# Splitting one GpSimd power into two, and twenty unread identity matmuls ahead of a tile's transposes, in a conv-attention and expert kernel

## The reference

```python
x = _L0_conv_ref(x, ...)        # group norm, qkv, 4-head softmax attention over 1024 pixels, residual
t = _to_tokens(x)               # 2 x 1024 tokens of 128 channels
t = t + _L1_attn_ref(_ln_t(t), ...)   # linear attention, 8 heads
t = t + _L1_ffn_ref(_ln_t(t), ...)    # the experts
```

```python
probs = softmax(xt @ Wr + br)
top_p, top_idx = top_k(probs, 2);  weights = top_p / top_p.sum(-1)
xn = (xt - mu) * rsqrt(var + 1e-5)
xe = xn * ln_g[e] + ln_b[e]
y  = gelu(xe @ W1[e] + b1[e]) @ W2[e] + b2[e]
out = sum over the two experts of weights * y
```

## Time and profile before

| | us |
|---|---|
| median of 3 runs | 366.21 (363.61, 366.21, 366.22) |
| the profiled execution | 364.42 |
| its span, first to last instruction | 362.7 |
| mean granted TensorE clock, share of full | 0.939 |

### The profile page before, as it was taken

One profiled execution on the slowest core, in us unless ns is written; L12 is line 12 of the kernel. 1 busy time (PEld: TensorE's weight loads), 2 busy tenths in 40 slices (PEclk: granted clock), 3 DMA queues, 4 the chain that ended last, 5 costly groups with the idle time before them and its releaser, 6 DMA issues.

```text
span 362.7 us, 6245 instructions
## 1 busy us (share of the span) xinstructions
PE 315.6 (87%) x1885; PEld 192.7 (53%) x1885; DVE 198.9 (55%) x617; ACT 194.1 (54%) x303; POOL 113.8 (31%) x190
## 2 busy tenths in 40 slices
PE   7979899999999998999999987697635499999996
PEld 3533433433333334435453254486534399999995
DVE  1586434474554844556447854766862057786510
ACT  1470566666666663656558620476532177777722
POOL 2073094000000000100030588007177835566540
PEclk9995989999999999999999999898858589999999
DMA  7069795744000005300000011300011422224215
GB/s 195 4 130 206 157 203 233 202 137 184 2 1 4 1 2 143 91 0 2 1 2 0 31 45 37 75 1 17 14 44 51 110 53 77 68 69 126 94 50 213
DMA packets 20541, 27.88 MB, mean 77 GB/s; under 512 B 3832, under 2 KB 14509, under 8 KB 20253
## 3 DMA queue, kind: packets, MB, share of 16 engines
q1 hardware_dynamic: 15800, 17.57, 18.1%
q0 software_dynamic: 3520, 9.39, 8.2%
q10 hardware_dynamic: 1188, 0.53, 0.6%
HBM read 11.15 MB, written 8.33 MB: 54 GB/s over the span
## 4 chain that ended last, share of the span: by engine, by line
PE 67%; DVE 12%; POOL 9%; issue 7%; ACT 3%; DMA 1%; DVEq 0%; POOLq 0%; ACTq 0%
PE ps L885 15%; PE ps L1104 9%; PE ps L1084 9%; POOL expert_in L507 7%; PE ps L847 7%; PE ps L866 5%; DVE above L1217 4%; PE ps L727 2%; PE ps L827 2%; PE ps L943 2%; PE ps L767 2%; PE ps L799 2%; PE ps L1063 1%; DVE pm L1220 1%; PE ps L958 1%
## 5 line engine op out<-in xcount | busy, mean ns | idle before, releaser
L575 ACT ACTIVATE probs<-ps 128x1024 f32<-128x1024 f32 x64 | 65.3, 1021 | 34.7 <-PE ps L866 34.6
L885 PE MATMUL ps<-probs,vT 128*32 128x512 f32 x256 | 68.3, 609 | 0.1
L885 PE MATMUL ps<-probs,ones 128*32 128x512 f32 x256 | 68.3, 609 | 0.0
L1217 DVE CUSTOM_DVE_ANT_0 above<-ps,above 128x512 f32<-128x512 f32 x56 | 38.7, 690 | 39.8 <-PE ps L847 38.0
L443 POOL TENSOR_TENSOR rstd<-ve,minus_half 128x1 f32<-128x1 f32 (+2 forms) x6 | 10.3, 1724 | 152.6 <-DVE ve L1259 83.3
L1084 PE MATMUL ps<-w,GT 128*128 x312 | 44.5, 288 | 9.8 <-ACT GT L705 9.5
L1104 PE MATMUL ps<-XTT,w1s 128*128 128x128 f32 x312 | 45.2, 292 | 4.3 <-issue 4.2
L513 POOL DMA_INDIRECT token_out<-Y,yidx x39 | 37.7, 966 | 33.1 <-DVE Y L1530 27.2
L568 ACT ACTIVATE above<-ps 128x512 f32<-128x512 f32 x56 | 33.6, 599 | 25.6 <-PE ps L827 25.6
L1084 PEld LDWEIGHTS ps<-w,GT 128*128 128x128 f32 x312 | 40.1, 201 | 11.5 <-issue 11.4
L866 PE MATMUL ps<-Qs,Ks 98*128 98x512 f32 x128 | 43.9, 424 | 0.7 <-issue 0.7
(11 more groups left out here) (221 smaller groups left out, 431.3 us busy)
## 6 DMA issues: line engine op xcount, KB each, us to landing
XR<-expert_in SPq DMA_DIRECT2D x39, 65.0 KB, 1.9
Qs<-q_hi SPq DMA_DIRECT2D x16, 128.0 KB, 2.7
w<-in_L_ffn_W SPq DMA_DIRECT2D x1, 2048.0 KB, 8.3
w<-in_L_ffn_W SPq DMA_DIRECT2D x8, 256.0 KB, 4.4
YG<-token_out SPq DMA_DIRECT2D x8, 256.0 KB, 3.9
Ks<-k_hi SPq DMA_DIRECT2D x14, 128.0 KB, 2.9
expert_in<-zeros POOLq DMA_DIRECT2D x1, 1300.0 KB, 5.5
expert_in<-zeros POOLq DMA_DIRECT2D x1, 1235.0 KB, 8.0
```

What stands on the lines that cost most here:

```text
L575: nc.scalar.activation(probs[:, s % 3, :], bank(2 + 2 * (s % 2), 2), ACT.Exp).then_inc(exp_done, 1)
L885: last = nc.tensor.matmul(bank(6 + o % 2)[i * HD:(i + 1) * HD, :], w, probs[:, s % 3, hd * HALF:(hd + 1) * HALF], start=kt == 0, stop=kt = ...
L1217: nc.vector.tensor_tensor_reduce(above[:, n % 2, :], bank(base), above[:, n % 2, :], scale=1.0, scalar=-3.0e38, op0=ALU.add, op1=ALU.max, ...
```

## The change

Three things are done.

1. `rsqrt` issues one instruction of 8 values for each row instead of one instruction of 16 values for two rows. Each raises `rstd_ready` by one, so the waits count further: `v_gates` waits for the first row alone, `v_shift` for the second.
2. Image 1's indirect transfers are counted on two semaphores, the first eight on one and the last eight on another. SP waits for both before tile 9, as before.
3. TensorE, behind `down(8)` and ahead of the transposes of tiles 9 and 10, waits for `slots` of both images and for the first eight transfers of image 1, and then issues `keep_busy(20, 0)`, into bank 0.

```diff
+    WARM = 20
@@
-        scattered = [sem(f"scattered{b}") for b in range(B)]
+        scattered = [sem(f"scattered{i}") for i in range(B + 1)]
@@ SP
                 if t in (0, OWN):
-                    sp.wait_ge(scattered[int(t == OWN)], 16 * 2 * J)
+                    if t == 0:
+                        sp.wait_ge(scattered[0], 16 * 2 * J)
+                    else:
+                        sp.wait_ge(scattered[1], 16 * J)
+                        sp.wait_ge(scattered[2], 16 * J)
@@ GpSimd, rsqrt
-                nc.gpsimd.tensor_tensor(rstd[:, i:i + rows, 0:columns], ve[:, i:i + rows, 0:columns],
-                                        minus_half[:, 0:rows, 0:columns], ALU.pow).then_inc(rstd_ready, 1)
+                for r in range(i, i + rows):
+                    nc.gpsimd.tensor_tensor(rstd[:, r, 0:columns], ve[:, r, 0:columns], minus_half[:, 0, 0:columns],
+                                            ALU.pow).then_inc(rstd_ready, 1)
@@ GpSimd, scatter
-                                                X2[:, b, j, :], None).then_inc(scattered[b], 16)
+                                                X2[:, b, j, :], None).then_inc(scattered[b + b * (2 * j // J)], 16)
@@ TensorE, expert_step
                 if s == OWN:
                     down(s - 1)
+                    pe.wait_ge(slots_ready, B)
+                    pe.wait_ge(scattered[1], 16 * J)
+                    keep_busy(WARM, 0)
                     x_transpose(s)
                     x_transpose(s + 1)
@@ DVE, norm_apply
-                dve.wait_ge(rstd_ready, n + 1)
+                dve.wait_ge(rstd_ready, n + 1 + (n - B) // 2)
@@ DVE, v_shift
-                dve.wait_ge(rstd_ready, B + 2 * b + 2)
+                dve.wait_ge(rstd_ready, B + 3 * b + 3)
@@ DVE, v_gates
-                dve.wait_ge(rstd_ready, B + 2 * b + 2)
+                dve.wait_ge(rstd_ready, B + 3 * b + 2)
```

## The result

| | before | after |
|---|---|---|
| median, us | 366.22 (363.61 to 366.39, 4 runs) | 371.66 (371.26 to 373.60, 4 runs) |
| profiled execution, us | 364.42 | 371.58 |
| its span, us | 362.7 | 369.8 |
| mean granted clock | 0.939 | 0.949 |

The ratio is 1.0176, 95% interval 1.0119 to 1.0234: slower by more than the 1% that can be told from no change. It is that of the means of the executions, 372.05 and 365.61, which differ by 6.4 us; the two medians alone differ by 5.4 us, a ratio of 1.015. The forecast was 370.1 us, the range 366.5 to 373.5.

What follows compares the result with a forecast made beforehand. The chain was 67% TensorE, which idled 9.20 us for tile 9's rows and restarted at half clock. Power -0.55, later transposes +8.0 and warm clock -2.4 gave +5.0 on 365.1: 370.1 us, range 366.5 to 373.5.

Steps and rivals of the forecast that it cites:

- The twenty matmuls: TensorE behind tile 8: 0.86 us each, 17.2 us in all, delaying tile 9's transposes from 285.8 to 293.8, +8.0 us.
- such a late return: Rival's small form: the full clock returns late, some 3 us of the twenty run at half; 371.6 us, nearly all of 6%.
- The warm clock: Tile 9's transposes to tile 11's first product at full clock: 4.15 us against 6.5 before, a gain of 2.4 us.
- T + 3.1: T is the start of tile 9's transposes; ACT's gelu for tile 9 was to end 3.1 us after it.
- The Trainium skill's rule: Prices a throttled stretch at length times one minus the clock's share; behind the gap 3.1 us back, sum +4.3 us.
- the reason that I gave: From tile 9's transposes: ACT's and DVE's steps lie between TensorE's and gain nothing from its clock, so 2.4 us, not 3.1.
- The power apart: Image 1's logits: first row ready 1.26 us earlier, but DVE's shift waits for the second, so slots come 0.55 us earlier.
- my base of 365.1 us: Mean of the four executions of the kernel before, to which the forecast added its +5.0 us.
- the cover: Rival at the gap before tile 9: a matmul costs 0.43 us, twenty end before the rows; some 362.2 us, 5%.
- fell in the twenty: Rival: the clock falls or starts at half in the twenty matmuls; 371.6 us, or some 390 if half throughout; 6%.
- lost behind them: Rival: the twenty run as priced but tile 9's transposes at half clock, 2.4 us not given back; 372.5 us, 4%.
- The last case: Rival: first eight transfers land late, the twenty start late, or the power gives no head start (then 370.7 us); 2%.

Runs made afterwards that it cites:

- ten_two: Changed kernel with ten identity matmuls instead of twenty, plus two single ones in TensorE's gaps in image 1's routing; median 362.28 us, 0.9900 of the kernel before.
- twenty_only: Changed kernel with the power of 16 values in one instruction as before, the twenty matmuls kept; median 373.50 us, 1.0204 of the kernel before.

## Why the prediction was right

**The twenty matmuls: right, but for their start.** I priced one at 0.86 us from the attention product's rows and they cost 0.867. The place behind tile 8, the free wait for the eighth transfer, the full clock throughout and the in-order wait of the transposes came as written. The distance grew by 8.20 us against +8.0. Within it a term that I had put at nothing is 0.4 us: behind the idle time of the routing the clock came back later than before. Tile 8's second product stands 7.30 us behind tile 5's, before 6.90, and the twenty start that much later. Before, the clock was back in the stretch from 272 to 273, some 3 us behind the start of tile 5's second product (269.12); here it is some 4 us behind (270.19):

```profile
273.00:274.00 1.00, 1.00 (x7) 1.00 (x7) 0.00 (x0) 0.00 (x0) 0.84 (x1) 0.50 0.20 67
274.00:275.00 1.00, 1.00 (x10) 1.00 (x10) 0.82 (x2) 0.15 (x1) 0.69 (x2) 0.98 0.21 67
```

I had named such a late return for the twenty themselves, and not for the tiles ahead of them. The experiments with 10, 14, 20 and 30 show that what counts is what lies past the landing, in full.

**The warm clock: right in mechanism, 0.5 us too large.** It gave 1.85 us and not 2.4; every kernel whose matmuls reach the landing, or end less than 0.8 us ahead of it, has 4.67 to 4.73 us from the transposes to tile 11, those without a warm clock 6.4 to 6.6. The term that I mis-sized is the way of tile 9 through DVE. I had the gelu end at T + 3.1, and it ends here:

```profile
298.56 0.63 ACT L711 ACTIVATE GT<-H 128x512 f32<-128x512 f32 x1 [1.21 <-DVE H L1551]
```

That is 299.19, T + 3.54. DVE began its addition at 297.83, when the first product had ended at 297.69: 2.2 us behind the transposes and not 1.8. The Trainium skill's rule (TensorE: Matmul & The Clock Gate, Terms) would have given back 3.1 us; the measured 1.85 lies further from it than my estimate. The trace agrees with the reason that I gave: TensorE waits for ACT twice in these 4.67 us, 0.50 and 0.53 us.

**The power apart: the wrong step.** I wrote that the distance from the power to the first transfer shrinks by 0.55 us, held at that by the second row on DVE. It changed by +0.08 in this execution and by -0.3 to +0.1 in all with the split and no extra matmuls. The rows of GpSimd and DVE do look as forecast, beside the earlier trace rows:

```profile
246.82 3.28 POOL L449 TENSOR_TENSOR rstd<-ve,minus_half 128x8 f32<-128x8 f32 x2 [19.34 <-DVE ve L1270]
```

```profile
248.59 0.22 DVE L1359 TENSOR_TENSOR lg<-ps,rstd 128x64 f32<-128x64 f32 x1 [0.34 <-POOL rstd L449]
...
250.13 0.17 DVE L1350 SCALAR_TENSOR_TENSOR nm<-lmv,rstd 128x8 f32<-128x8 f32 x1 [0.54 <-POOL rstd L449]
250.95 0.69 DVE L1551 TENSOR_TENSOR H<-ps,b1T 128x512 f32<-128x512 f32 x1 [0.65 <-issue]
```

The logits wait 0.34 us instead of 1.60, the shift 0.54, and tile 3's addition stands 4.13 us behind the power instead of 4.70. But that wait isn't what holds the routing. I stopped at DVE, and didn't follow the counts, for which DVE waits, back to TensorE. There, in the changed kernel:

```profile
255.47 2.04 PE L1113 MATMUL ps<-XTT,w1s 128*128 128x128 f32 x8 [0.68 <-issue]
...
257.84 0.63 PE L1008 MATMUL ps<-mask,ones 128*128 128x64 f32 x2
```

The product starts 1.2 us earlier relative to the power than before and takes 0.9 us longer. The clock had fallen at 253 to 254 after TensorE's gaps in the routing, where before it had fallen at 251 to 252 and was full again at 255 to 256. The clock's rows there, two of the kernel before and then one of this:

```profile
251.00:252.00 1.00, 0.66 (x4) 0.69 (x5) 0.93 (x6) 0.98 (x2) 0.78 (x2) 0.82 0.01 0
255.00:256.00 1.00, 0.61 (x5) 0.44 (x5) 0.39 (x3) 0.59 (x2) 0.00 (x0) 0.97 0.00 0
```

```profile
253.00:254.00 1.00, 0.89 (x6) 0.90 (x7) 0.97 (x15) 1.00 (x4) 0.72 (x2) 0.78 0.19 66
```

The clock was not in my sum at this place at all. That the half clock takes the gain is shown by ten_two. It costs only where it meets the product and the counts: in twenty_only, with the power in one instruction, the granted clock was full from 245 to 265, and the distance is 16.50 us, as before the change with half clock at 252 to 255. What decides in which of the neighbouring gaps it falls, I can't say from these runs.

**The number.** With the three measured terms the sum is +6.4 instead of +5.0, and on my base of 365.1 us that is 371.5, beside 371.66. All three terms were off in the same direction, by 0.6, 0.2 and 0.5 us; the range had room for it. That the two medians differ by 5.4 us, close to my 5.0, is luck of a few executions: the means differ by 6.4, as the distances do.

The rivals: the cover did not hold, and the clock neither fell in the twenty nor was lost behind them. The last case, to which I gave 2%, came true in a small form: the power had no head start, worth 0.6 us, and the twenty started another 0.4 us late for the clock in tiles 5 to 8. One slip in the rivals: twenty matmuls at the half clock would take 37.8 us by the earlier trace rows, not 37.4.

## What to carry to other kernels

Filler for a warm clock has a length, and it is that of the gap: read the gap from the trace, price the filler from a row of the same shape and type at the full clock, and let it end before the data lands. Half a microsecond of slack costs nothing, and each microsecond too many costs one.

When an instruction on the path gets earlier, follow every engine that the path returns to, with its clock at that moment. A stretch that starts earlier can run at the other clock and give the gain back.

## What was not expected of the hardware

With four matmuls TensorE was idle from 279.6 on, and yet the granted clock stood at full for some five microseconds more; it fell within the stretch from 284 to 285, a fraction of a microsecond before the transposes started at 285.09:

```profile
283.00:284.00 1.00, 0.00 (x0) 0.00 (x0) 0.00 (x0) 0.00 (x0) 0.72 (x3) 1.00 0.19 66
284.00:285.00 1.00, 0.00 (x0) 0.00 (x0) 0.00 (x0) 0.00 (x0) 0.72 (x3) 0.87 0.61 125
285.00:286.00 1.00, 0.89 (x2) 0.37 (x2) 0.00 (x0) 0.33 (x1) 1.00 (x2) 0.50 0.76 201
```

In the kernel before TensorE was idle from 277.2 on, and the clock was at half from 279 on, less than two microseconds later:

```profile
278.00:279.00 1.00, 0.00 (x0) 0.00 (x0) 0.00 (x0) 0.00 (x0) 0.69 (x2) 0.98 0.20 67
279.00:280.00 1.00, 0.00 (x0) 0.00 (x0) 0.00 (x0) 0.00 (x0) 0.69 (x2) 0.50 0.11 37
```

So how long the full clock outlasts the work differs between these two by a factor of more than two. The filler of four lost by less than a microsecond; whether a filler that short keeps the clock in other executions isn't shown.

Two powers of 8 values in a row took 3.28 us together, 1.64 each, where one alone took 1.68 and one of 16 values 2.94: apart they cost 0.34 us, not the 0.42 forecast.
